# Drains that signal in place of matmuls in the edge loop of a graph attention kernel

## The chip, the cores and the metric

The kernel runs on one core of a Trainium2 chip. The metric is the device time of one execution in microseconds (us); the time before is the median of three runs.

## What is computed

One layer of graph attention, followed by a mixture of experts; only the first half matters here. `h` is a projection of the 6250 normalised nodes to 8 heads of 32, and there are 200000 edges, sorted by `dst`:

```python
h_src = h[src]
h_dst = h[dst]
alpha = jnp.einsum('ehd,hd->eh', h_src, a_src) + jnp.einsum('ehd,hd->eh', h_dst, a_dst)
enc = jax.nn.relu(edge_attr @ edge_W.T + edge_b).reshape(-1, H, D)
alpha = alpha + jnp.sum(enc * h_dst, axis=-1)
alpha = jnp.where(alpha >= 0, alpha, 0.2 * alpha)
amax = jax.ops.segment_max(alpha, dst, num_segments=n)
ex = jnp.exp(alpha - amax[dst])
denom = jax.ops.segment_sum(ex, dst, num_segments=n)
attn = ex / jnp.maximum(denom[dst], 1e-10)
out = jax.ops.segment_sum(h_src * attn[..., None], dst, num_segments=n)
```

`x + out + bias` then goes through the experts and a last normalisation.

## The kernel before

The program has four parts: a prologue that projects the nodes and sorts edges into blocks, the edge loop, a merge of the blocks' sums, and the experts. The change lies in `edge_loop` alone.

A block is 128 rows of four edges each; all edges of a row have the same destination. Four blocks make a step, and the loop has 110 steps, written out, with two sets of buffers (`RING`) that alternate. Each engine has its own hand-written order, and semaphores hold them together. For block `b` of step `q` (its running number is `n`):

- SP loads the block's attributes (`load_attr`, L888), the window of 128 node rows from which destinations are taken (`load_windows`, L909), the places of the rows in it (`load_places`, L902) and flags, two steps ahead, and stores the sums (`store`, L916).
- POOL gathers the source rows, four gathers of 128 rows per block (`gather`, L989). The gathers into a buffer wait until `weighted` of two steps before is done, and until `near` of the block before is there (L997, L1001).
- PE, in `front` (L1026): four matmuls make the encodings of the block's four edges per row (`p_enc`, L1038, two pairs), and one, the pick, takes the rows' destination nodes out of the window (`p_pick`, L1045). A float32 matmul is two in the profile. In `add_up` (L1057), four float32 matmuls (eight in the profile) add the weighted source rows by destination (`p_sum`, L1066).
- ACT copies the pick (`near`, L1146) and the sums (`sums`, L1167), makes the one-hot matrices, and the exponentials that are the weights (L1154, L1155), which wait until all sums of the step before are done.
- DVE multiplies encodings by `near` and reduces them (`front`, L1212), makes the scores once the step's gathers have landed (`scores`, L1227), finds the maximum of each run of rows (`scan`, L1242, between two transposes on PE: `turn_rows` and `turn_back`), and multiplies source rows by weights (`weigh`, L1261).

The fronts run one step ahead of the rest. PE's order in a step `q` with next step `n` (L1077) is: `turn_rows(q)`, `front(n, 1)`, `add_up` of block 2 of the step before, `turn_back(q)`, `front(n, 2)`, `add_up` of block 3 of the step before, `front(n, 3)`, `add_up(q, 0)`, `front` of block 0 of the step after next, `add_up(q, 1)`. DVE's is: `scores(q)`, `front(n, 0)`, `weigh` of block 2 of the step before, `scan(q)`, `front(n, 1)`, `weigh` of block 3 of the step before, `fall(q)`, `front(n, 2)`, `weigh(q, 0)`, `front(n, 3)`, `weigh(q, 1)`.

Before the change, the second matmul of each encoder pair increments `enc`, the pick increments `picked`, and the last matmul of the sums increments `summed`. DVE waits for `enc` before each of its two products of a block, ACT waits for `picked` and `summed`, and SP's `load_attr` waits for `enc` before it overwrites the attributes.

Of the kernel before, what the change touches and what calls it, by code (L numbers as in the profile page):

```python
# [27 lines left out]
W = 4  # L28
SLOTS = P * W
Q = 16 // W  # L30
PAIRS = W // 2
# [13 lines left out]
ROW = D + H  # L45
# [30 lines left out]
def block_of(ap, t):  # L76

    return ap[t, :, :] if isinstance(t, int) else ap[bass.ds(t, 1), :, :].rearrange("o p n -> p (o n)")
# [720 lines left out]
def straight(k):  # L799
    return Step(k).of(k // RING, k % RING)  # L800


def edge_loop(nc, a, scr, keep):

    with Scope(nc) as m:
        attrT = m.sb("attrT", [KE, RING, Q, SLOTS], BF16)
        flags = m.sb("flags_in", [Q * H, RING, P + 1])
        win = m.sb("win", [P, RING, Q, TABROW])
        src = m.sb("src_in", [P, RING, Q, W, TABROW])
        apart = m.sb("apart", [P, P])  # L810
        hot = m.sb("hot", [P, RING, Q, P])
        hotT = m.sb("hotT", [P, RING, Q, P])
        near = m.sb("near", [P, RING, Q, TABROW])
        prod = m.sb("prod", [P, W, D])
        dots = m.sb("dots", [P, RING, Q, W, H])
        raw = m.sb("raw", [P, Q, W, H])
        full = m.sb("full", [P, Q, W, H])
        score = m.sb("score", [P, Q, W, H])
        row_top = m.sb("row_top", [P, Q, H])
        run = m.sb("run", [Q * H, P])  # L820
        tops = m.sb("tops", [Q * H, 2, P])
        below = m.sb("below", [P, Q, W, H])
        weighted = m.sb("weighted", [P, Q, W, ROW])
# [22 lines left out]
        p_enc = [m.ps(f"p_enc{i}", [P, 2, D]) for i in range(4)]  # L846
        p_pick = m.ps("p_pick", [P, 512])
        p_turn = m.ps("p_turn", [P, 512])
        p_sum = [m.ps(f"p_sum{i}", [P, 512]) for i in range(2)]
        p_near = p_pick[:, 0:TABROW]  # L850
# [8 lines left out]
        s_win = [m.sem(f"s_win_loaded{i}") for i in range(RING)]  # L859
        s_src = [[m.sem(f"s_gathered{i}{q}") for q in range(Q)] for i in range(RING)]  # L860
        s_stored = [m.sem(f"s_sums_stored{i}") for i in range(RING)]
        names = """waited_by_pe waited_by_pool ones_set zeros_set apart hot far hotT picked near enc prod dots raw full score row_top rowT run tops back below
            weight own_weight weighted merge summed sums tops_kept biased moved rows_out rows_up rows_turned attr_made table_stored item items_made items_stored""".split()
        s = {n: m.sem("l_" + n) for n in names}

# [2 lines left out]
        def steps(body, last):  # L868


            for k in range(STEPS - 2):
                body(straight(k))
            last()
# [13 lines left out]
        def _(sp):  # L887
            def load_attr(q):  # L888
                if q.since(RING):
                    sp.wait_ge(s["enc"], PAIRS * Q * (q.prev().s))  # L890
                cols = scr["block_attr"].rearrange("c (n e) -> n c e", e=Q * SLOTS)
                v = block_of(cols, q.s)
                for j in range(3):
                    sp.dma_start(attrT[KA * j:KA * (j + 1), q.par, :, :].rearrange("c q e -> c (q e)"), v).then_inc(s_attr[q.par], 16)
# [129 lines left out]
        @block.tensor  # L1024
        def _(pe):
            def front(q, b):  # L1026

                n = q.s * Q + b
                some = b or q.since(1)
                if b == 0:  # L1030
                    pe.wait_ge(s_attr[q.par], 48 * (q.turn + 1))
                for half in range(PAIRS):
                    if PAIRS * b + half >= len(p_enc) or q.since(1):
                        pe.wait_ge(s["prod"], PAIRS * n + half + 1 - len(p_enc))
                    for j in range(2):
                        k = 2 * half + j
                        slots = attrT[:, q.par, b, :].rearrange("c (r k) -> c k r", k=W)[:, k, :]
                        last = nc.tensor.matmul(p_enc[(PAIRS * b + half) % len(p_enc)][:, j, :], slots, keep["expander"][:, :], start=True, stop=True)  # L1038
                    last.then_inc(s["enc"], 1)
                if some:  # L1040
                    pe.wait_ge(s["near"], n)
                if b == 0:
                    pe.wait_ge(s["hotT"], q.s + 1)
                    pe.wait_ge(s_win[q.par], 16 * Q * (q.turn + 1))
                nc.tensor.matmul(p_near, hotT[:, q.par, b, :], win[:, q.par, b, :], start=True, stop=True).then_inc(s["picked"], 1)  # L1045

            def turn_rows(q):
                if q.since(1):
                    pe.wait_ge(s["below"], q.s)
                nc.tensor.transpose(p_rowT, row_top[:, :, :].rearrange("p q h -> p (q h)"), keep["ident"][:, :]).then_inc(s["rowT"], 1)  # L1050

            def turn_back(q):
                pe.wait_ge(s["tops"], q.s + 1)
                nc.tensor.sem_inc(s["waited_by_pe"], 1)
                nc.tensor.transpose(p_back, tops[:, q.par, :], keep["ident"][0:Q * H, 0:Q * H]).then_inc(s["back"], 1)  # L1055

            def add_up(q, b):  # L1057
                n = q.s * Q + b
                pe.wait_ge(s["hot"], n + 1)
                pe.wait_ge(s["weighted"], n + 1)  # L1060
                if b == 0:
                    pe.wait_ge(s["own_weight"], q.s + 1)
                if b > 1 or q.since(1):
                    pe.wait_ge(s["sums"], n - 1)
                for k in range(W):
                    last = nc.tensor.matmul(p_sum[b % 2][:, 0:ROW], hot[:, q.par, b, :], weighted[:, b, k, :], start=(k == 0), stop=(k == W - 1))  # L1066
                last.then_inc(s["summed"], 1)

            def turn_table(group, k):

                if group:
                    pe.wait_ge(s["rows_out"], group)
                if group or k:
                    pe.wait_ge(s["rows_turned"], (W + 1) * group + k)
                nc.tensor.transpose(p_turn[:, P:2 * P], ro[:, k, :], keep["ident"][:, :]).then_inc(s["rows_up"], 1)

            def body(q, ahead=2):  # L1077

                n, before = q.next(), q.prev()
                group, u = divmod(q.s - RING, turn)  # L1080
                pe.wait_ge(s["row_top"], q.s + 1)
                if 0 <= group < GROUPS - 1 and 0 <= u - TURNED_AT <= W:
                    turn_table(group + 1, u - TURNED_AT)
                turn_rows(q)
                if ahead:
                    front(n, 1)
                if q.since(1):
                    add_up(before, 2)
                turn_back(q)
                if ahead:  # L1090
                    front(n, 2)
                if q.since(1):
                    add_up(before, 3)
                if ahead:
                    front(n, 3)
                add_up(q, 0)
                if ahead > 1:
                    front(n.next(), 0)
                add_up(q, 1)

            def last():
                body(straight(STEPS - 2), 1)
                body(straight(STEPS - 1), 0)
                for b in range(2, Q):
                    add_up(straight(STEPS - 1), b)

            for k in range(W + 1):
                turn_table(0, k)
            for b in range(Q):
                front(straight(0), b)  # L1110
            front(straight(1), 0)
            steps(body, last)
# [98 lines left out]
        def _(dve):  # L1211
            def front(q, b):  # L1212

                n = q.s * Q + b
                dve.wait_ge(s["near"], n + 1)
                if n:
                    dve.wait_ge(s["dots"], n)
                for half in range(PAIRS):
                    dve.wait_ge(s["enc"], PAIRS * n + half + 1)
                    nc.vector.scalar_tensor_tensor(prod[:, 2 * half:2 * half + 2, :], p_enc[(PAIRS * b + half) % len(p_enc)][:, :, :], 0.0,  # L1220
                                                   near[:, q.par, b, 0:D].unsqueeze(1).broadcast_to([P, 2, D]),
                                                   ALU.max, ALU.mult).then_inc(s["prod"], 1)
                dve.wait_ge(s["prod"], PAIRS * n + PAIRS)
                nc.vector.tensor_reduce(dots[:, q.par, b, :, :].rearrange("p k h -> p (k h)"),  # L1224
                                        prod[:, :, :].rearrange("p k (h d) -> p (k h) d", h=H), AX.X, ALU.add).then_inc(s["dots"], 1)
# [787 lines left out]
def edge_part(nc, a, scr, whole):  # L2013
    with Scope(nc) as m:
# [17 lines left out]
        def over_planes(rows, n):  # L2032
# [9 lines left out]
            gain=over_planes(1, GROUPS * P), parts=over_planes(P, ITILES * ROW).rearrange("p (t q) -> p t q", t=ITILES),  # L2042
        )
        edge_loop(nc, a, scr, keep)
        merge_blocks(nc, scr, keep)

# [16 lines left out]
```

## Time and profile before

| | us |
|---|---|
| median of three runs | 2976.41 (2975.30 to 2976.63) |
| the profiled execution | 2971.36 |
| its span, first to last instruction | 2969.6 |
| DVE busy | 2268.7 (76%) |
| PE busy | 2234.4 (75%) |
| POOL busy | 1860.1 (63%) |
| ACT busy | 1025.9 (35%) |

The edge loop lies between about 169 us and 2452 us of the span. A busy share is an average over stages: the times of instructions and the waits ahead of them are read by line. In a trace, PE is the matmuls, PEld the loads of their weights, and a name with a q at its end (PEldq, SPq) the queue of that engine, where waits, drains and DMA issues stand. The ends of matmuls are modelled. "Issue" as the releaser of an idle time means that the profile shows nothing that the engine waited for.

### The profile page before, as it was taken

What the parts mean: (1) busy time and instruction counts of PE and PEld (TensorE: products, weight loads), DVE (VectorE), ACT (ScalarE), POOL (GpSimd) and SP (SyncE); (2) the same over time, 40 slices, a digit from 0 to 9 for tenths busy, and PEclk for the clock granted to TensorE, in tenths of its full rate; (3) what the DMA queues carried; (4) which work ended last, traced back from release to release, by engine and by line L of the source; (5) the groups of instructions that cost most, each with busy time, mean ns of one, the idle gap of its engine ahead of it and who ended that gap; (6) DMA issues with size and microseconds to landing.
All of it is one profiled execution on the core that took longest, in us unless ns stands there. A gap on an engine that the chain in (4) does not pass through costs nothing. (4 is left out here: it accounts for less than half of the span.)

```text
span 2969.6 us, 35673 instructions
## 1 busy us (share of the span) xinstructions
PE 2234.4 (75%) x8662; PEld 1521.2 (51%) x8662; DVE 2268.7 (76%) x3626; ACT 1025.9 (35%) x2822; POOL 1860.1 (63%) x1993
## 2 busy tenths in 40 slices
PE   0947777787787777777877877777777762789997
PEld 0624545454454444444544544444444441778886
DVE  7848898988888998888889889888887883713224
ACT  2713333333333333333333333333333330623332
POOL 2257777777777777777777777777777753371000
PEclk9958788878889888888898888898897885589999
DMA  8466566657666666667666666566666642110000
GB/s 265 175 152 188 172 189 180 178 167 211 190 179 185 190 179 182 177 175 216 177 186 191 181 180 186 167 187 202 186 191 174 191 129 62 53 32 14 21 18 33
DMA packets 240722, 468.64 MB, mean 158 GB/s; under 512 B 57466, under 2 KB 148268, under 8 KB 240288
## 3 DMA queue, kind: packets, MB, share of 16 engines
q0 software_dynamic: 90000, 262.14, 32.0%
q1 hardware_dynamic: 149696, 204.29, 21.9%
q8 instruction: 60, 0.98, 0.1%
q14 instruction: 118, 0.97, 0.1%
q10 hardware_dynamic: 848, 0.26, 0.0%
HBM read 379.04 MB, written 87.41 MB: 157 GB/s over the span
## 5 line engine op out<-in xcount | busy, mean ns | idle before, releaser
L1004 POOL DMA_INDIRECT src_in<-t_node_rows,row_src x1760 | 1684.3, 957 | 572.5 <-issue 501.6
L1066 PE MATMUL p_sum<-weighted,hot 128*128 128x264 f32 x3520 | 1095.1, 465 | 368.7 <-issue 253.3
L1066 PEld LDWEIGHTS p_sum<-weighted,hot 128*128 128x128 f32 x3520 | 770.7, 228 | 679.8 <-issue 367.1
L1220 DVE SCALAR_TENSOR_TENSOR prod<-p_enc,near 128x512 f32<-128x512 f32 x880 | 561.2, 678 | 77.8 <-ACT near L1146 74.7
L1270 DVE TENSOR_TENSOR weighted<-src_in,p_turn 128x1024 f32<-128x1024 f32 x440 | 533.7, 1214 | 97.9 <-PE p_turn L1055 67.9
L1224 DVE TENSOR_REDUCE dots<-prod 128x32 f32<-128x1024 f32 x440 | 536.8, 1220 | 15.2
L1167 ACT COPY sums<-p_sum 128x264 f32<-128x264 f32 x440 | 164.5, 374 | 742.1 <-PE p_sum L1066 737.3
L1146 ACT COPY near<-p_pick 128x272 f32<-128x272 f32 x440 | 169.8, 386 | 553.4 <-PE p_pick L1045 553.4
L1045 PE MATMUL p_pick<-win,hotT 128*128 128x272 f32 x880 | 360.2, 495 | 0.6 <-issue 0.6
L1038 PE MATMUL p_enc<-expander,attrT 30*128 30x256 bf16 x1760 | 307.9, 300 | 5.4 <-DMA attrT<-t_block_attr 5.4
L1038 PEld LDWEIGHTS p_enc<-expander,attrT 30*128 30x128 bf16 x1760 | 174.0, 121 | 117.2 <-issue 75.6
L1045 PEld LDWEIGHTS p_pick<-win,hotT 128*128 128x128 f32 x880 | 145.3, 207 | 103.4 <-issue 101.8
L1932 DVE TENSOR_TENSOR acc<-acc,p_y 128x256 f32 (+1 forms) x49 | 20.6, 421 | 218.8 <-PE p_y L1747 216.3
L1737 PE MATMUL p_up<-x2T,w 128*128 (+2 forms) x800 | 176.1, 379 | 9.5 <-DMA b<-in_L_ffn_b 9.5
L1124 ACT ACTIVATE apart<-node_at,row_near 128x128 f32<-128x128 f32 x440 | 176.4, 401 | 0.0
L1747 PE MATMUL p_y<-w,act_h 128*128 128x256 f32 x784 | 173.1, 379 | 0.0
L1737 PEld LDWEIGHTS p_up<-x2T,w 128*128 128x128 f32 x800 | 151.5, 193 | 30.3 <-DMA b<-in_L_ffn_b 9.6
L1747 PEld LDWEIGHTS p_y<-w,act_h 128*128 128x128 f32 x784 | 148.9, 190 | 20.2
L1812 ACT ACTIVATE act_h<-p_up,b 128x256 f32<-128x256 f32 (+1 forms) x200 | 91.7, 468 | 159.5 <-PE p_up L1737 158.5
L1050 PE MATMUL p_turn<-ident,row_top 128*32 128x128 f32 x110 | 32.7, 297 | 144.7 <-DVE row_top L1240 144.5
L1128 ACT ACTIVATE hot<-apart 128x128 f32<-128x128 f32 x440 | 136.2, 310 | 14.0
L1232 DVE TENSOR_TENSOR raw<-dots,src_in 128x128 f32<-128x128 f32 x110 | 32.1, 292 | 105.0 <-DMA src_in<-t_node_rows,row_src 104.0
(350 smaller groups left out, 1651.7 us busy)
## 6 DMA issues: line engine op xcount, KB each, us to landing
win<-t_node_rows SPq DMA_DIRECT2D x440, 136.0 KB, 3.1
t_block_sums<-sums SPq DMA_DIRECT2D x110, 528.0 KB
hotT<-t_block_places SPq DMA_DIRECT2D x110, 256.0 KB, 4.4
src_in<-t_node_rows,row_src POOLq DMA_INDIRECT x1760, 2.8
attrT<-t_block_attr SPq DMA_DIRECT2D x330, 36.0 KB
t_node_rows<-out_rows SPq DMA_DIRECT2D x49, 136.0 KB, 1.7
x<-in_x SPq DMA_DIRECT2D x4, 1536.0 KB, 24.9
out_x<-x SPq DMA_DIRECT2D x48, 128.0 KB
```

The lines of the kernel that those rows point to most:

```text
L1004: pool.indirect_dma_start(src[:, q.par, b, k, :], None, scr["rows"], bass.IndirectOffsetOnAxis(ap=row_src[:, group % 2, k, at_block:at_blo ...
L1038: last = nc.tensor.matmul(p_enc[(PAIRS * b + half) % len(p_enc)][:, j, :], slots, keep["expander"][:, :], start=True, stop=True)
L1045: nc.tensor.matmul(p_near, hotT[:, q.par, b, :], win[:, q.par, b, :], start=True, stop=True).then_inc(s["picked"], 1)
L1066: last = nc.tensor.matmul(p_sum[b % 2][:, 0:ROW], hot[:, q.par, b, :], weighted[:, b, k, :], start=(k == 0), stop=(k == W - 1))
L1124: nc.scalar.activation(apart[:, :], keep["node_at"][:, :], ACT.Abs, bias=row_near[:, group % 2, at_block:at_block + 1]).then_inc(s["apart" ...
L1146: nc.scalar.copy(near[:, q.par, b, :], p_near).then_inc(s["near"], 1)
L1167: nc.scalar.copy(sums[:, q.par, b, :], p_sum[b % 2][:, 0:ROW]).then_inc(s["sums"], 1)
L1220: nc.vector.scalar_tensor_tensor(prod[:, 2 * half:2 * half + 2, :], p_enc[(PAIRS * b + half) % len(p_enc)][:, :, :], 0.0, near[:, q.par, b ...
L1224: nc.vector.tensor_reduce(dots[:, q.par, b, :, :].rearrange("p k h -> p (k h)"), prod[:, :, :].rearrange("p k (h d) -> p (k h) d", h=H), A ...
L1270: nc.vector.tensor_tensor(heads(weighted[:, b, :, 0:D]), heads(src[:, q.par, b, :, 0:D]), spread(p_weight[:, b, :, :], HD), ALU.mult).then ...
L1737: last = nc.tensor.matmul(p_up[n % 4][:, 0:cols], w1[:, k, i, f * P:(f + 1) * P], x, start=(i == 0), stop=(i == 1))
L1747: last = nc.tensor.matmul(p_y[u][:, :], act_h[:, b, n, u * P:(u + 1) * P], w2[:, k, f, :], start=(n == 0), stop=(n == TOPK * hidden - 1))
```

## The change

The encoder's matmuls no longer increment anything; the semaphore `enc` is gone. Behind the pick of each block, and behind the sums of each block, PE gets a drain, an instruction of its queue that is over when the matmuls ahead of it are, and it increments `picked` or `summed` in place of the last matmul. DVE no longer waits for `enc`; the pick stands behind the encoder's matmuls on PE, so `near`, for which DVE waits, comes after them. `load_attr` on SP waits for all picks of the step two before instead of all its encodings. The order of the matmuls, and of all other work on every engine, is as before. There are 440 drains of each kind.

```diff
@@ -887,7 +887,7 @@
             def load_attr(q):
                 if q.since(RING):
-                    sp.wait_ge(s["enc"], PAIRS * Q * (q.prev().s))
+                    sp.wait_ge(s["picked"], Q * q.prev().s)
                 cols = scr["block_attr"].rearrange("c (n e) -> n c e", e=Q * SLOTS)
...
@@ -1035,14 +1035,14 @@
                     for j in range(2):
                         k = 2 * half + j
                         slots = attrT[:, q.par, b, :].rearrange("c (r k) -> c k r", k=W)[:, k, :]
-                        last = nc.tensor.matmul(p_enc[(PAIRS * b + half) % len(p_enc)][:, j, :], slots, keep["expander"][:, :], start=True, stop=True)
-                    last.then_inc(s["enc"], 1)
+                        nc.tensor.matmul(p_enc[(PAIRS * b + half) % len(p_enc)][:, j, :], slots, keep["expander"][:, :], start=True, stop=True)
                 if some:
                     pe.wait_ge(s["near"], n)
                 if b == 0:
                     pe.wait_ge(s["hotT"], q.s + 1)
                     pe.wait_ge(s_win[q.par], 16 * Q * (q.turn + 1))
-                nc.tensor.matmul(p_near, hotT[:, q.par, b, :], win[:, q.par, b, :], start=True, stop=True).then_inc(s["picked"], 1)
+                nc.tensor.matmul(p_near, hotT[:, q.par, b, :], win[:, q.par, b, :], start=True, stop=True)
+                nc.tensor.drain().then_inc(s["picked"], 1)
...
@@ -1063,8 +1063,8 @@
                 for k in range(W):
-                    last = nc.tensor.matmul(p_sum[b % 2][:, 0:ROW], hot[:, q.par, b, :], weighted[:, b, k, :], start=(k == 0), stop=(k == W - 1))
-                last.then_inc(s["summed"], 1)
+                    nc.tensor.matmul(p_sum[b % 2][:, 0:ROW], hot[:, q.par, b, :], weighted[:, b, k, :], start=(k == 0), stop=(k == W - 1))
+                nc.tensor.drain().then_inc(s["summed"], 1)
...
@@ -1216,7 +1216,6 @@
                 for half in range(PAIRS):
-                    dve.wait_ge(s["enc"], PAIRS * n + half + 1)
                     nc.vector.scalar_tensor_tensor(prod[:, 2 * half:2 * half + 2, :], p_enc[(PAIRS * b + half) % len(p_enc)][:, :, :], 0.0,
```

## Rows read from the trace of the kernel before

**Rows 1.** The gathers' line: ns min/median/max; idle before it by releaser, times.
```profile
L1004 POOL DMA_INDIRECT src_in<-t_node_rows,row_src x1760: 940/946/2484, 168.7 to 2422.9; - x196
...
  issue: 501.6, 1604
  DVE weighted L1270: 38.4, 106
  ACT near L1146: 30.9, 49
```

**Rows 2.** Waits of DVE: engine, line, releaser, total us, times, longest.
```profile
DVE raw L1232 <- DMA src_in<-t_node_rows,row_src: 104.0, 66, 7.1
DVE prod L1220 <- ACT near L1146: 74.7, 130, 7.8
DVE weighted L1270 <- PE p_turn L1055: 67.9, 81, 3.2
```

**Rows 3.** Timeline around one held gather: start, duration, engine, instruction, idle before.
```profile
1719.16 0.94 POOL L1004 DMA_INDIRECT src_in<-t_node_rows,row_src  x1 [0.30 <-issue]
...
1720.10 0.39 ACT L1146 COPY near<-p_pick 128x272 f32<-128x272 f32 x1 [1.84 <-PE p_pick L1045]
...
1721.29 0.94 POOL L1004 DMA_INDIRECT src_in<-t_node_rows,row_src  x1 [1.19 <-ACT near L1146]
```

**Rows 4.** Timeline, sums: inside one group, and the loop's last four groups.
```profile
1517.12 1.72 PE L1066 MATMUL p_sum<-weighted,hot 128*128 128x264 f32 x7
...
2444.64 7.36 PE L1066 MATMUL p_sum<-weighted,hot 128*128 128x264 f32 x32 [1.73 <-DVE weighted L1270]
...
2452.04 0.38 ACT L1167 COPY sums<-p_sum 128x264 f32<-128x264 f32 x1 [1.40 <-PE p_sum L1066]
```

**Rows 5.** The sums' line on PE: duration of one, ns min/median/max.
```profile
L1066 PE MATMUL p_sum<-weighted,hot x3520: 386/386/780, 204.4 to 2451.6; 128*128 128x264 f32 x196
```

**Rows 6.** Waits of SP's queue.
```profile
SPq L894 <- PE p_enc L1038: 6.4, 3, 3.1
```

**Rows 7.** The barrier behind the loop: PE's drain, ns, start us.
```profile
L805 PEldq DRAIN  x1: 3028/3028/3028, 2449.0 to 2449.0; - x1
```

**Rows 8.** Timeline of part of one step at the full clock.
```profile
1511.15 1.21 DVE L1270 TENSOR_TENSOR weighted<-src_in,p_turn 128x1024 f32<-128x1024 f32 x1
...
1512.46 2.02 PE L1066 MATMUL p_sum<-weighted,hot 128*128 128x264 f32 x8 [2.12 <-issue]
...
1514.41 0.24 PE L1055 MATMUL p_turn<-ident,tops 32*128 32x32 f32 x1
...
1515.02 0.73 PE L1045 MATMUL p_pick<-win,hotT 128*128 128x272 f32 x2
...
1516.82 2.02 PE L1066 MATMUL p_sum<-weighted,hot 128*128 128x264 f32 x8 [1.07 <-ACT hot L1128]
...
1518.77 0.62 PE L1038 MATMUL p_enc<-expander,attrT 30*128 30x256 bf16 x4
```

**Rows 9.** PE's queue ahead of the transpose of `tops`.
```profile
L1054 PEldq EVENT_SEMAPHORE  x110: 51/51/51, 197.8 to 2436.4; - x110
```

**Rows 10.** Timeline of PE in a stretch at the lower clock.
```profile
1816.16 3.86 PE L1066 MATMUL p_sum<-weighted,hot 128*128 128x264 f32 x8 [2.12 <-issue]
...
1821.04 1.28 PE L1045 MATMUL p_pick<-win,hotT 128*128 128x272 f32 x2
1822.11 3.18 PE L1066 MATMUL p_sum<-weighted,hot 128*128 128x264 f32 x8
```

**Rows 11.** Stretches (that sum, two steps, the loop): length, busy us by engine, PEclk.
```profile
1816.20:1820.00 3.80, 3.80 (x9) 2.50 (x10) 2.98 (x5) 0.00 (x0) 2.89 (x4) 0.50 0.46 129
1770.96:1792.73 21.77, 17.18 (x58) 11.08 (x58) 18.73 (x27) 7.11 (x21) 16.22 (x17) 0.76 0.61 174
1853.24:1872.65 19.41, 13.26 (x58) 8.52 (x58) 18.67 (x28) 7.11 (x21) 14.72 (x16) 1.00 0.67 196
300.00:2300.00 2000.00, 1540.34 (x5669) 977.68 (x5670) 1743.91 (x2515) 691.95 (x2045) 1493.91 (x1560) 0.85 0.64 184
```

More of the change, by code:

```diff
@@ L861, in edge_loop @@
         s_stored = [m.sem(f"s_sums_stored{i}") for i in range(RING)]
-        names = """waited_by_pe waited_by_pool ones_set zeros_set apart hot far hotT picked near enc prod dots raw full score row_top rowT run tops back below
+        names = """waited_by_pe waited_by_pool ones_set zeros_set apart hot far hotT picked near prod dots raw full score row_top rowT run tops back below
             weight own_weight weighted merge summed sums tops_kept biased moved rows_out rows_up rows_turned attr_made table_stored item items_made items_stored""".split()
```

## The prediction

> **What bounds the kernel now.** I read POOL's edge gathers first, the costliest line of the page [rows 1]: 1760 gathers (L1004) from 168.7 us to 2422.9 us, and nearly all of POOL's idle time ahead of them is "issue", the pause that it makes after every one. A gather that waits for nothing starts 1.25 us after the one before it, 0.95 of work and 0.30 of pause [rows 3], so the sixteen of a step need 20.0 us and all 1760 need 2200 us; the stretch is 2254 us long. POOL paces the edge loop, which is three quarters of the span, and all that faster matmuls could win there is those 54 us. What can be lost is not capped.
>
> The second thing to see is how close the other engines run. POOL waited 106 times for `weighted` and 49 times for `near` [rows 1], and DVE waited for a gather before only 66 of the 110 steps [rows 2]; in the other 44 the gathers had landed and DVE itself was late. A step is 20.5 us on average (2254 / 110) against POOL's 20.0. Two loops of nearly equal length run side by side, POOL's and the chain through DVE, PE and ACT, and a delay on the second shows wherever it is the later one.
>
> Where PE enters that chain is in DVE's waits [rows 2]: 81 times for the transpose of `tops` (L1055, 67.9 us), 130 times for `near` (74.7 us). The last four gathers of a step wait for the `near` of that step's third block: one copy ended at 1720.49, the gather started at 1721.29, after 1.19 us of idle and 0.80 us behind its release [rows 3].
>
> **What the signals cost now.** Seven matmuls of one group with no signal among them take 1.72 us, and the eight of a group take 2.02 [rows 4, 8]. A run of 32, four groups with three signals inside, takes 7.36: 24 more in 5.34 us is 222.5 ns each, against (1.72 - 0.386) / 6 = 222.3 without a signal, where 0.386 is a single matmul of the line [rows 4, 5]. Three signals cost 5 ns together. The Trainium skill speaks for the change here: TensorE: Matmul & The Clock Gate, "The cost: per-tile semaphore tail", gives about 26 ns for each increment, by which three signals fewer in each of 440 blocks would be an estimated 34 us. The trace does not agree (2 ns a signal), and the sum goes on without that figure.
>
> **Taking the encoder's signals away: nothing.** DVE's wait for the encoder stood beside its wait for `near`, which is made from a pick that stands behind the encoder's four matmuls on PE; so the encoder was never the later one. On SP it held `load_attr` 3 times for 6.4 us in the whole run [rows 6], and SP's next loads of the same step wait for `picked` anyway, which is what `load_attr` waits for now. I take zero; the bounds are a gain of those 6.4 us and a loss of as much.
>
> **What a drain costs.** The trace has no drain inside the loop, but the barrier that closes the loop has one on PE: it started at 2449.0 us and lasted 3.028 us, to about 2452.03 [rows 7], while the last matmul ended at 2452.00 and ACT, on that matmul's own signal, started at 2452.04 [rows 4]. So the drain is over some 0.03 to 0.05 us behind the matmuls, and what waits for its signal starts about 0.05 us later than it would now.
>
> The larger part is what stands behind the drain. Today the next group begins before the last one has ended: p_sum runs from 1512.46 to 1514.48, the transpose begins at 1514.41; the next p_sum ends at 1518.84, the encoder begins at 1518.77; both 0.07 us early [rows 8]. With the drain PE's queue issues nothing until the array is empty. How long PE needs from a release to its first matmul is in the same rows: `weighted` ends at 1512.36, p_sum starts at 1512.46, 0.10 us. I take 0.04 for the drain and 0.06 to 0.10 for the start, so an encoder behind a drained sum starts some 0.12 us after it instead of 0.07 before: 0.19 us later. Ahead of the transpose of `tops` stands a semaphore instruction of 51 ns as well, which today runs while the sum does [rows 9]: 0.25 us. The bounds are 0.17 (0.10 and 0.07, no more) and 0.4.
>
> Eight drains fall into a step. The one behind the sum of the third block is followed by the transpose of `tops`, the encoder and the third pick: all come 0.25 us later, and `near`, by the pick's own drain, 0.30. The one behind the sum of the fourth block delays ACT's weights by 0.05 and the last encoder by 0.19. The one behind the first block's sum delays an encoder that is used a step later, and the one behind the second's ends in PE's wait for `row_top`: hidden, and at 0.25 us each if that cover went. The four behind picks are followed by sums, which mostly wait for `weighted`: after the pick that ended at 1515.75 PE stood 1.07 us until 1516.82 [rows 8], so the restart is covered. Where that cover is gone, as at 1822.11, where a sum began 0.2 us before the end of its pick [rows 10], such a drain costs up to 0.4 us.
>
> **The sum.** In the 44 steps in which DVE is the late one it loses 0.25 (transpose) + 0.05 (weights) + 0.19 (last `near`) = 0.49 us: 21.6 us. In the 49 places where POOL waited for `near`, 0.30 us: 14.7 us. In the remaining 17 steps POOL has slack: zero. At the end of the loop four sums run one behind the other [rows 4], with three drains between them now, and two more lie on the way there: about 1.5 us, all on the path. Together 37.8 us. The profiled execution took 2971.36 us, 1.8 more than its span; it becomes 3009. The median of the runs shown is 5.05 us above that execution, so I expect 3014 us.
>
> The low bound takes the drains as visible only where POOL waited for `near`, at 0.17 us each: 8 us, 2985. I see no gain to set below it but the two that are rivals. The high bound lies in the clock's case and is set at 3055.
>
> **The rivals.**
> The clock falls: slower, but by twice as much. At 1814 PE stood 2.12 us, then ran at 1.2 GHz (granted clock 0.50): a p_sum took 3.86 us where 2.02 is usual, the pick 1.28, all without a pause, and the sum after that, 3.18 us, was partly at 2.4 GHz again [rows 10, 11]. It came back after a stretch without a gap, and each drain cuts a gap into such stretches. Steps at a mean granted clock of 0.76 and 1.00 took 21.8 and 19.4 us, which is 10 us for a whole unit; the loop's mean is 0.85 [rows 11]. If it falls by 0.03, the 110 steps lose a further 33 us: 3047. Against it: the long wait that it falls after stays as it is. The Trainium skill has a like case (TensorE: Matmul & The Clock Gate, "A second HAM failure mode: psum-queue depth-cycling"): small idles between groups of matmuls made the clock swing. Whether gaps as short as a drain's do so, no row here shows.
>
> POOL hides it. If the 0.5 us between a step and POOL's 20.0 takes up the delays, what is left is the 8 us of the low bound and up to a third of the sum: 2980 to 2996. Against it stand the 44 and the 49.
>
> Faster. If a signal on a matmul holds back what follows it, PE gains at every encoder and every sum, and the restart behind a drain is covered by waits like the 1.07 us above, then part of POOL's 54 us comes back; a tenth of them is 2971. It decides the sign from the point at which a signal costs PE more than the 0.19 us of a restart. Rows 4 and 5 leave 2 ns for one.
>
> The drains do nothing. If PE's queue goes on behind them, the time stays within 6 us. Against it: the barrier's drain ended just behind the last matmul, 3 us after its start.
>
> **How the numbers follow.** The forecast (2996 to 3031) 0.52, the clock (3031 to 3080) 0.22, POOL hides it 0.13, nothing changes 0.09, faster 0.04. The range 2985 to 3055 holds the forecast, most of the clock's case and two thirds of POOL's: 0.8. A change of 0.2%, 6 us, is about what a measurement of this kernel tells from none: slower 0.87, same 0.09, faster 0.04.
>
> **What would show it.** Right: in a step's timeline the transposes and encoders start 0.1 us or more behind a sum's end instead of 0.07 ahead; `near` starts 0.05 us later behind its pick; DVE's waits for the transpose of `tops` grow by some 20 us; POOL's waits for `near` grow by 15 us or more; gathers keep 0.95 us. Wrong: an encoder still starts under a sum (the drain holds nothing), a gap of 0.4 us or more behind every sum (the drain is undersized), or a mean granted clock in the loop away from 0.85 (the size comes from the clock).

## The result, and the profile after

| | before | after |
|---|---|---|
| median, us | 2975.30 (2972.45 to 2976.63, five runs) | 3008.43 (3006.58 to 3022.14, five runs) |
| ratio | | 1.0125 (95%: 1.011 to 1.014) |
| profiled execution, us | 2971.36 | 3022.14 |
| gathers, first to last start, us | 168.7 to 2422.9 | 170.1 to 2467.0 |
| mean granted clock of the span | 0.848 | 0.843 |

The change makes the kernel slower by 1.25%, 37 us. The execution that was profiled is the longest of the five; the other four had granted clocks of 0.847 to 0.849. Its waits therefore add up to more than the typical 37 us.

First the gathers' line and the waits of DVE, which answer to [rows 1] and [rows 2]: in the first fence the releaser, us and times; in the second the line, its releaser, us, times, longest. The last fence is one more row of DVE's waits in the trace of before.

```profile
L1004 POOL DMA_INDIRECT src_in<-t_node_rows,row_src x1760: 940/946/2481, 170.1 to 2467.0; - x196
...
  issue: 495.2, 1572
  ACT near L1146: 80.1, 96
  DVE weighted L1269: 39.1, 91
```

```profile
DVE raw L1231 <- DMA src_in<-t_node_rows,row_src: 95.7, 52, 7.1
DVE prod L1219 <- ACT near L1146: 94.0, 135, 7.5
DVE weighted L1269 <- PE p_turn L1055: 75.6, 82, 3.7
DVE weighted L1269 <- ACT p_turn L1154: 56.2, 52, 3.9
```

```profile
DVE weighted L1270 <- ACT p_turn L1154: 29.2, 47, 2.3
```

A gather still takes 0.946 us. POOL waits for `near` 96 times and 80 us instead of 49 times and 31. These rows hold the pause of 0.30 us that POOL makes after every gather as well: in the trace of before only 14 of the 49 waits are longer than 0.35 us, and they come to 16 us beyond the pause; after, it is 45 waits and 51 us. That is 35 of the 43 us by which the stretch from the first to the last gather has grown. DVE waits 19 us longer for `near`, 27 us longer for ACT's weights and only 8 us longer for the transpose of `tops`. DVE waits less for gathers: the chain through DVE, PE and ACT has become the later one more often.

This is PE's timeline of one step and a half after the change (start, duration, instruction, count, idle before); it answers to [rows 8] and [rows 10].

```profile
1510.41 3.86 PE L1066 MATMUL p_sum<-weighted,hot 128*128 128x264 f32 x8 [0.33 <-issue]
1514.49 1.01 PE L1038 MATMUL p_enc<-expander,attrT 30*128 30x256 bf16 x4 [0.23 <-issue]
1515.44 1.28 PE L1044 MATMUL p_pick<-win,hotT 128*128 128x272 f32 x2
1516.94 3.06 PE L1066 MATMUL p_sum<-weighted,hot 128*128 128x264 f32 x8 [0.23 <-issue]
...
1521.94 2.02 PE L1066 MATMUL p_sum<-weighted,hot 128*128 128x264 f32 x8 [0.23 <-DVE weighted L1269]
1524.19 0.21 PE L1055 MATMUL p_turn<-ident,tops 32*128 32x32 f32 x1 [0.23 <-issue]
1524.24 0.60 PE L1038 MATMUL p_enc<-expander,attrT 30*128 30x256 bf16 x4
1524.77 0.72 PE L1044 MATMUL p_pick<-win,hotT 128*128 128x272 f32 x2
1526.19 2.02 PE L1066 MATMUL p_sum<-weighted,hot 128*128 128x264 f32 x8 [0.69 <-DVE weighted L1269]
1528.29 0.62 PE L1038 MATMUL p_enc<-expander,attrT 30*128 30x256 bf16 x4
```

Neither a sum nor what stands behind a sum begins under the group before it any more. The transpose, which began 0.07 us before the end of its sum, begins 0.23 us behind it; the encoder at 1528.29 begins 0.08 us behind the sum that ends at 1528.21, and the encoder of the first block, at 1514.49, 0.23 us behind its sum. In all 107 steps with the usual order of groups these three gaps are the same to 0.01 us. At the lower clock the sum behind a pick, which began 0.2 us early at 1822.11 before, begins at 1516.94, 0.22 us behind the pick that ends at 1516.72. The loop's end shows the bare price: the run of four sums that took 7.36 us [rows 4] is now four runs.

```profile
2494.01 2.02 PE L1066 MATMUL p_sum<-weighted,hot 128*128 128x264 f32 x8 [1.75 <-DVE weighted L1269]
2496.26 2.02 PE L1066 MATMUL p_sum<-weighted,hot 128*128 128x264 f32 x8 [0.23 <-DVE weighted L1269]
2498.50 2.02 PE L1066 MATMUL p_sum<-weighted,hot 128*128 128x264 f32 x8 [0.23 <-issue]
2500.75 2.02 PE L1066 MATMUL p_sum<-weighted,hot 128*128 128x264 f32 x8 [0.23 <-issue]
```

From start to start it is 2.25 us, where eight matmuls at 222.5 ns are 1.78: 0.47 us for each drain between two groups that had followed each other without a gap. These four runs end at 2502.77, 8.76 us after they began; 1.40 us is what three drains added there.

### The profile page after: what moved, and what is told of

Same layout as the page of the kernel before. It is cut to its first block and busy times, and to the rows that moved or that the text cites. A ratio compares the mean times of both kernels' runs of the same rounds, so it can differ in the third digit from the quotient of the medians.

```text
span 3020.4 us, 36552 instructions
## 1 busy us (share of the span) xinstructions
PE 2276.2 (75%) x8662; PEld 1514.6 (50%) x8662; DVE 2269.5 (75%) x3626; ACT 1027.6 (34%) x2822; POOL 1859.0 (62%) x1993
## 5 line engine op out<-in xcount | busy, mean ns | idle before, releaser
L1044 PE MATMUL p_pick<-win,hotT 128*128 128x272 f32 x880 | 369.2, 506 | 0.6 <-issue 0.6
L1154 ACT ACTIVATE p_turn<-below 128x128 f32<-128x128 f32 x110 | 30.9, 281 | 225.1 <-PEq L1067 225.1
```

## The experiments

Each run is given as the ratio to the kernel before, measured beside it on the same chip, and in us of 2976. Where an expectation speaks of a replay, that is a calculation: the durations and waits recorded in the trace of before, followed again with the drains' gaps put in.

| run | ratio (95%) | us |
|---|---|---|
| enc_off | 1.0003 (0.9993 to 1.0013) | +1 |
| drain_pick | 1.0060 (1.0041 to 1.0079) | +18 |
| drain_sum | 1.0053 (1.0037 to 1.0069) | +16 |
| drain_mute | 1.0123 (1.0104 to 1.0142) | +37 |
| pick_third | 1.0053 (1.0039 to 1.0067) | +16 |
| pick_rest | 1.0027 (1.0017 to 1.0036) | +8 |
| sum_third | 1.0056 (1.0042 to 1.0069) | +17 |
| sum_rest | 1.0037 (1.0024 to 1.0051) | +11 |
| early | 0.9987 (0.9976 to 0.9999) | -4 |
| early_drain | 1.0111 (1.0090 to 1.0132) | +33 |
| three_gathers | 0.9592 (0.9575 to 0.9609) | -121 |
| three_drain | 0.9708 (0.9679 to 0.9736) | -87 |

**One part at a time.** `enc_off` takes only the encoder's signals away; `drain_pick` and `drain_sum` put one of the two kinds of drain back; `drain_mute` has all drains, but they signal nothing. The edits, against the changed kernel:

```diff
 enc_off: both edits below;  drain_pick: the second;  drain_sum: the first
-                nc.tensor.matmul(p_near, ...)
-                nc.tensor.drain().then_inc(s["picked"], 1)
+                nc.tensor.matmul(p_near, ...).then_inc(s["picked"], 1)
...
-                nc.tensor.drain().then_inc(s["summed"], 1)
+                last.then_inc(s["summed"], 1)
 drain_mute: as enc_off, and behind each of the two
+                nc.tensor.drain()
```

> Only the encoder's signals are gone; pick and sums signal by their last matmul, and there are no drains. Theory (a signal on a matmul costs 2 ns, the drains cost everything): 2975 us, within 6 us of before. Rival (signals on matmuls hold PE back): 10 us or more faster than before, and the change's cost is then larger than it looks by as much.

> The change with drains behind the picks alone; sums signal by their last matmul. Theory by the terms of the prediction: the pick's drain delays near by 0.05 us and is else hidden by PE's wait for weighted, so 49 x 0.05 + 44 x 0.05 = 5 us, 2980; where a sum begins under its pick at the lower clock the drain costs 0.4 us, which a replay of the recorded waits puts at up to 15 us in all, 2990. Rival (the clock carries the loss): the size follows the mean granted clock of the run, not the kind of drain.

> The change with drains behind the sums alone; picks signal by their matmul. Theory: this is the larger part, 0.25 us on the transpose and the third near in each step that is exposed, 23 to 32 us: 2998 to 3007. Rival (drains of both kinds cost the same, because any gap on PE costs): half of the 33 us, 2992.

> All 880 drains are there, but the matmuls keep their signals on pick and sums, and the drains signal nothing. Theory (the gap behind a drain costs, the later signal little): 3 to 5 us less than the change, 3003 to 3006. Rival (the later signal costs most): near before, 2975 to 2985.

Measured: +1, +18, +16 and +37 us. The encoder's signals cost nothing (-2 to +4 us). The drains cost all of it: with the matmuls' own signals kept and the drains only standing there, the loss is that of the change, so the later signal is at most a few us of it. (ACT's copy of a pick begins 0.057 us behind the pick's end where the drain signals, and 0.037 us where the matmul does: medians of the copies that waited for it, after and before.) And the two kinds cost the same within what can be told, which was the rival's figure for the sums and not mine: drains behind picks were expected to cost 5 to 15 us and cost 18, drains behind sums 23 to 32 and cost 16.

The two leave different marks. Waits of DVE and POOL (line, releaser, total us, times, longest) with drains behind picks alone:

```profile
DVE weighted L1269 <- PE p_turn L1055: 63.9, 77, 3.5
...
DVE weighted L1269 <- ACT p_turn L1154: 44.4, 48, 4.2
...
POOL src_in L1004 <- ACT near L1146: 27.7, 44, 3.1
```

and with drains behind sums alone:

```profile
DVE weighted L1268 <- PE p_turn L1054: 77.0, 87, 3.7
...
POOL src_in L1004 <- ACT near L1145: 61.5, 104, 2.8
...
DVE weighted L1268 <- ACT p_turn L1153: 34.1, 60, 3.9
```

Two things limit what these rows can carry. The profiled execution of `drain_pick` is the shortest of its six and that of `drain_sum` the longest; and `enc_off`, which takes as long as before, has 63.4, 35.6 and 33.0 us in the same three rows, so that 7 us in a row mean nothing. Behind sums it is the path that was named: POOL's wait for `near` doubles (30.9 us before; beyond POOL's pause 16 us before and 30 here), the wait for the transpose grows by 9 us. Behind picks neither moves, and DVE waits 15 us longer for ACT's weights than before (9 longer than in `enc_off`); these wait for the sum of the fourth block. PE's timeline of the picks' run shows where that sum is delayed:

```profile
1501.90 1.27 PE L1044 MATMUL p_pick<-win,hotT 128*128 128x272 f32 x2
1503.41 3.13 PE L1066 MATMUL p_sum<-weighted,hot 128*128 128x264 f32 x8 [0.23 <-issue]
...
1521.78 1.27 PE L1044 MATMUL p_pick<-win,hotT 128*128 128x272 f32 x2
1523.29 3.42 PE L1066 MATMUL p_sum<-weighted,hot 128*128 128x264 f32 x8 [0.23 <-issue]
```

This is the third pick of a step, at the lower clock, with the next sum, that of the fourth block of the step before, ready to go; in the trace of before that sum begins under the pick in 59 of 108 steps, and under another pick only once.

**One place at a time.** If that is so, the third pick and the third block's sum carry nearly everything. The edit chooses who signals by block:

```diff
 pick_third (pick_rest: (0, 1, 3)), with signals on the sums' matmuls; last is the pick's or the sums' last matmul
...
-                nc.tensor.drain().then_inc(s["picked"], 1)
+                (nc.tensor.drain() if b in (2,) else last).then_inc(s["picked"], 1)
...
 sum_third (sum_rest: (0, 1, 3)), with signals on the picks' matmuls
-                nc.tensor.drain().then_inc(s["summed"], 1)
+                if b in (2,):
+                    last = nc.tensor.drain()
+                last.then_inc(s["summed"], 1)
```

> Of all drains only the one behind each step's third pick is left (110 of them). The run with drains behind picks alone lost 17 us, and its trace put it into DVE's wait for ACT's weights. Theory: it comes from the third pick, behind which, at the lower clock, the fourth block's sum of the step before follows without a pause; the weights wait for that sum: 12 to 17 us slower than before, 2989 to 2994. Rival (each pick's drain costs alike): a quarter, 4 us, 2981.

> Drains behind the first, second and fourth pick of a step, 330 of them. Theory: covered by PE's waits for weighted, 0 to 5 us slower than before, 2977 to 2982. Rival (alike): three quarters, 13 us, 2990.

> Of all drains only the one behind the sum of each step's third block is left. Theory: the transpose of tops, the third pick and POOL's last gathers of the step hang on it: nearly all that drains behind sums cost, 12 to 18 us slower than before, 2989 to 2995. Rival (alike): 4 us, 2981.

> Drains behind the sums of the first, second and fourth block of a step. By the prediction's term the fourth delays the last near by 0.19 us in 44 steps, 8 us slower than before, 2985. By the replay of recorded waits ACT, busy with the weights, hides it: 0 to 2 us, 2978. Rival (alike): 12 us, 2989.

Measured: +16, +8, +17 and +11 us. A quarter of the drains, those at the third block, cost as much as all four of their kind; "each costs alike" is refuted (4 us expected for a quarter). DVE's wait for ACT's weights agrees: 48.9 us in the trace of `pick_third`, 35.6 in that of `pick_rest`. But the others are not free: 8 us and 11 us. Sums without the third were put at 8 us by the prediction's term for the last `near`, and at 0 to 2 by the replay; the replay was wrong. The parts also do not add: 17 and 11 us of sums make 16 together, beyond the intervals (0.93% with 0.19% against 0.53% with 0.16%), while 16 and 8 us of picks against 18 are within them. A delay in one place may hide a later one in the same step, or be hidden by it; that is not shown.

**Is it POOL's wait for `near`?** The third front can stand in front of the sum for which PE waits, and the fourth one place earlier as well. If the drains cost mainly through POOL's wait for `near`, that move takes the wait and most of the cost away.

```diff
                 if ahead:
                     front(n, 1)
+                    front(n, 2)
                 if q.since(1):
                     add_up(before, 2)
                 turn_back(q)
                 if ahead:
-                    front(n, 2)
+                    front(n, 3)
                 if q.since(1):
                     add_up(before, 3)
-                if ahead:
-                    front(n, 3)
                 add_up(q, 0)
```

ACT's `move_near(n, 2)` moves in front of `move_sums(before, 2)`, and `move_near(n, 3)` into its old place.

> The kernel before (signals on the matmuls) with PE's fronts of the third and fourth block one place earlier: the third in front of the sum of the third block of the step before, where PE waits for weighted, the fourth in front of the next sum; ACT's copies of near follow. Theory: POOL's wait for near (31 us, and 80 with the drains) hangs on the third front's place behind that sum and the transpose; with it moved the wait is gone: 15 to 50 us faster than before, 2927 to 2962. Rival (POOL's wait is only handed on, DVE or PE is next in the same place): 2970 to 2980.

> The same move of the two fronts in the changed kernel with all its drains. Theory: the drains cost through POOL's wait for near and through DVE's waits for the transpose and the weights; the first of these is gone, so the drains cost 10 to 20 us here instead of 33 to 37. Rival (any gap on PE costs, whatever stands behind it, or the clock does): 33 us or more above the same move without drains.

Measured: `early` is 4 us faster than before, at the edge of what can be told, and its granted clocks were higher (0.849 to 0.859, against 0.841 to 0.850 beside it), so that the new order may have won nothing; `early_drain` is 37 us slower than `early`. My theory fell twice. The waits of `early`:

```profile
DVE raw L1231 <- DMA src_in<-t_node_rows,row_src: 147.7, 78, 7.1
...
DVE weighted L1269 <- PE p_turn L1055: 86.6, 77, 3.5
...
DVE weighted L1269 <- ACT p_turn L1153: 48.4, 27, 4.2
...
POOL src_in L1004 <- ACT near L1145: 28.7, 63, 2.9
...
DVE prod L1219 <- ACT near L1145: 7.7, 1, 7.7
```

and of `early_drain`:

```profile
DVE weighted L1268 <- PE p_turn L1055: 127.2, 86, 3.4
...
POOL src_in L1004 <- DVE weighted L1268: 57.3, 104, 3.1
...
POOL src_in L1004 <- ACT near L1145: 48.1, 64, 2.9
```

The move took DVE's wait for `near` away (74.7 us to 7.7), and 44 us more came back as waits for gathers, 19 as waits for the transpose, 19 as waits for weights: handed on. POOL's wait for `near` beyond its pauses fell from 16 us to 10, and was not gone. With drains, the transpose, which still stands behind a drained sum, makes DVE wait 41 us longer. The cost is not tied to the path through `near`; it comes out on whichever path is left.

This pair also speaks on the clock: mean granted clocks were 0.855 and 0.862, higher with the drains than without, and the drains still cost 37 us. At like clocks the loss is there too: executions of `early` at 0.849 to 0.851 took 2975 to 2983 us, those of `early_drain` at 0.847 and 0.850 took 3024 and 3021 us. With drains behind sums alone the profiled clock was 0.852, above the 0.848 of before, at +16 us.

**Does POOL hide a part?** Three gathers of four, in the kernel before and in the changed one, leave POOL with time to spare. Both leave out the fourth edge of each row.

```diff
-                    for k in range(W):
+                    for k in range(W - 1):
                         pool.indirect_dma_start(src[:, q.par, b, k, :], ...)
...
-                    dve.wait_ge(s_src[q.par][b], 16 * W * (q.turn + 1))
+                    dve.wait_ge(s_src[q.par][b], 16 * (W - 1) * (q.turn + 1))
...
+            nc.vector.memset(src[:, :, :, W - 1, :], 0.0).then_inc(s["zeros_set"], 1)
```

> The kernel before with three of the four gathers of every block; the fourth edge of each row is left out of the computation (its source rows are zeros, set once), all other work is as it was. It takes a quarter of POOL's time away. Theory (POOL and the chain through DVE, PE and ACT run side by side at nearly equal length): the loop falls to the chain's length and no further, 80 to 110 us faster than before, 2870 to 2900, where POOL alone would give 550. Rival (POOL alone sets the pace): 300 us or more faster.

> The same with all drains of the change. Theory: POOL no longer hides any part of the drains' cost, so they cost 45 to 60 us over the run with three gathers, more than the 33 to 38 here. Rival (most of the drains' cost came through POOL's wait for near): 20 us or less. Rival (every gap counts as it is, POOL hides nothing now either): 33 to 38 us.

Measured: 121 us faster than before, and with the drains 87 us faster, a cost of 35 us (21 to 48 between the far ends of both intervals). A quarter of POOL's work is worth a fifth of what it would be if POOL alone set the pace (1760 / 4 gathers of 1.25 us are 550 us). The rows of three gathers:

```profile
POOL src_in L1004 <- DVE weighted L1270: 311.5, 148, 5.7
...
POOL src_in L1004 <- ACT near L1146: 215.8, 120, 3.1
...
DVE prod L1220 <- ACT near L1146: 69.6, 144, 4.8
...
DVE raw L1232 <- DMA src_in<-t_node_rows,row_src: 23.9, 31, 4.7
```

POOL now waits 527 us for the chain (446 beyond its pauses, where it was 23 before), and DVE for gathers only 24. The chain alone is 1.1 us a step shorter than the loop was, so POOL and the chain do run side by side, as the prediction read them. Part of the 1.1 us may be the array's clock, which was 0.871 to 0.878 here and 0.844 to 0.852 in the executions of before beside it: by the two steps of [rows 11], 10 us for a whole unit of clock, 0.026 is 0.26 us a step, an estimate. The drains' cost is 35 us with POOL out of the way and 37 with it: POOL hid nothing that can be measured, though the interval leaves room for some 13 us either way. The 45 to 60 us that I expected without it lie at the edge of the interval or outside.

## Why the prediction was right, and where it was not

The forecast was 3014 us, slower, and 3008 was measured; the ratio's 37 us stand against its 38. The sign, the cause and the size of one drain were right. The split of the total was not: about 36 us were put on the sums and nothing on the picks, and 16 and 18 were measured. That the total came out as it did is luck, two errors that cancelled.

**Signals cost nothing: right.** In the run of 32 matmuls the next one begins 222 or 223 ns after the last across a signal as elsewhere; taking 880 signals away was +1 us (-2 to +4). The prediction's "three signals fewer" in a block is a miscount, on which its sum does not rest: four leave the matmuls, and two of them come back on the drains. The rule of the Trainium skill (TensorE: Matmul & The Clock Gate, "The cost: per-tile semaphore tail"), some 26 ns for an increment, is a gain of 23 us for these 880 (an estimate by that page); no run shows it. These increments stand on matmuls that follow one another, not on small tiles that run side by side.

**The price of a drain: right in size.** 0.19 us was taken for an encoder behind a drained sum; it was 0.15 for the last one of a step (from 0.07 before the end to 0.08 behind it) and 0.30 for that of the first block. 0.25 was taken for the transpose; it was 0.30. 0.4 for a pick's drain without cover; it was 0.44 at the lower clock (from 0.21 before the pick's end to 0.23 behind it). The later signal was put at 0.05 us and was 0.02; in the total it cannot be told from zero, for muted drains cost as much. The loop's end was put at 1.5 us, and three drains took 1.40 there.

**Hidden behind picks: wrong.** This is the step that failed: "the four behind picks are followed by sums, which mostly wait for `weighted`". The step quoted from [rows 8] has that cover, but in 59 of 108 steps the third pick has none, and that is the pick behind which the sum stands that ACT's weights wait for. The prediction saw such a place [rows 10], priced it at 0.4 us and left it out of the sum. Drains behind picks cost 18 us, and 16 with the third pick's alone. The place should have been counted over the whole loop: 59 times 0.4 is 24 us, an upper bound, since not every delay need reach the end.

**The sums' term: too large.** About 36 us were expected and 16 measured. Its two places were right (in the run with drains behind sums POOL's wait for `near` beyond its pause grew by 14 us and the wait for the transpose by 9), as was the smaller part without the third block (8 us expected, 11 measured). What was wrong was to add 44 exposed steps and 49 exposed waits. The 49 of [rows 1] lie in 41 steps, and 21 of these are among the 44 in which DVE was late, so that the same step is charged twice; and 35 of the 49 are no longer than POOL's own pause, where the gather was not held. Which of the rest reaches the end is not shown.

**Two loops of equal length: right as a reading, wrong as a discount.** The prediction gave POOL 17 steps in which it hides the drains, what 44 and 49 leave of 110, which falls with that sum. In every arrangement that was tried, with POOL pacing, with the fronts moved, with POOL relieved, all drains together cost 35 to 37 us, 0.3 us a step. Why they come to the same sum in all three is not settled.

**The rivals.** The clock did not carry the loss: at like granted clocks it stands, as with `early` above. It does go with the spread between executions of one kernel: in every kernel here the longer ones had lower clocks on the whole (0.843 at 3022 us and 0.849 at 3007 and 3008 us after the change; 0.888 at 2872 us and 0.871 at 2894 us in `three_drain`). Which of the two causes the other was not tried. The Trainium skill's case of a swinging clock (TensorE: Matmul & The Clock Gate, "A second HAM failure mode: psum-queue depth-cycling") is not seen for gaps of 0.23 us: the mean granted clock was 0.843 to 0.849 with the drains, and 0.841 to 0.852 in the executions of before. "The drains do nothing" and "faster" are refuted by the change's own 37 us and by the drains put back one kind at a time.

**What was to be seen:** encoders and transposes behind the sum's end, yes; `near` 0.05 us later behind its pick, nearly (0.02); POOL's waits for `near` up by 15 us or more, yes (49, of which 35 beyond its pauses); gathers at 0.95 us, yes; DVE's wait for the transpose up by 20 us, no (8). The wait for ACT's weights (27 us more) was put at 0.05 us in 44 steps and does not stand in the prediction's list of what to watch.

## What to carry to other kernels

A signal on a matmul cost nothing here that could be measured; a drain in its place made the queue wait until the array was empty, and took up to 0.47 us wherever the next group was ready. Before a wait is called a cover, count in how many repetitions it is there: here it was missing in more than half (59 of 108), and just at the pick ahead of the sum that the weights wait for. Before two lists of waits are added, look whether they lie in the same steps, and take off the pause that the engine makes anyway. When a wait is moved away in a loop whose parts are of nearly equal length, expect it to come back under another name.

## What the runs showed of the hardware

Behind a drain PE stands idle 0.23 us when its next group is ready and has a semaphore instruction ahead of it, and 0.08 us behind a sum when it has none (1528.29; 0.079 to 0.082 in 107 steps). The 0.23 us is the same at either clock: it stands ahead of the sums at 2496.26 and 2498.50 and ahead of the encoder at 1514.49, behind a stretch that the windows view (length, busy us of PE, PEld, DVE, ACT, POOL, then PEclk) has at the lower level:

```profile
1510.50:1514.00 3.50, 3.50 (x8) 2.40 (x8) 3.42 (x4) 1.87 (x5) 2.07 (x3) 0.50 0.74 264
```

This idle time does not change with the array's clock; that it lies in PE's queue is the likely reading, and was not tried. No run put another instruction of the queue in the drain's place, so how much of the cost any further instruction there would have is open too.
